# Moving the low parts of two projection weights to GpSimd, with a new front order, in a fused attention and MoE kernel

## The chip, the cores and the metric

The kernel runs on one core of one Trainium2 chip. Its time is the device time of one execution in microseconds (us). Three runs took 939.1, 931.1 and 933.65 us, so the median is 933.65. A separate profiled execution took 935.56 us, of which the profile's span covers 933.7.

## The reference

```
xn = layernorm(x)                              # x: 4 x 512 tokens x 512
p  = xn @ W_in.T ; s_t = d*s_(t-1) + (1-d)*p_t # d = sigmoid(decay), a scan over tokens
a  = s @ W_out.T + bias
r  = softmax(xn @ wg_router.T)                 # 32 experts, top 6, weights renormalised
y  = sum over the chosen experts of w * (silu(xn@w_gate[e]) * (xn@w_up[e])) @ w_down[e]
sh = (silu(xn@ws_gate) * (xn@ws_up)) @ ws_down # shared expert, width 704
out = x + a + y + sh
```

## The kernel before, in words

**Split matmuls.** Every product is computed with three matmuls: an fp32 operand v is split into a high part (v rounded to fp32r, written by ACT as a copy) and a low part (v less the high part, a subtraction on DVE), and TensorE (PE) adds high x high, high x low and low x high. All copies share the profile's line L859, all subtractions L1573, and the three matmuls are L1256, L1257 and L1258. The profile names a buffer by its memory: `w_hi` also stands for the high parts of the projection weights, of the normalised input `xb` and of the scanned states `st`.

**The front** (0 to about 112 us). The 2,048 tokens are 16 tiles of 128 rows, and four batches of 4 tiles. Per tile: DVE measures mean and variance (`measure`, L1596 and L1599), ACT takes the root (`deviation`, L879), DVE the factors (`factors`, L1605 and L1606), ACT writes normalised rows for the transposes (`normalise`, L885) and a second, reordered copy for HBM (`reorder`, L893), PE transposes (`tile_T`, L1236), and DVE moves the result to SBUF (`tile_evac`, L1586). Per batch: ACT and DVE split the input (`xb_hi`, `xb_lo`), PE projects four column chunks (`in_proj`), ACT scales each (`q`, into two buffers), DVE scans it (`scan_of`, L1845), ACT and DVE split the states (`st_hi`, `st_lo`), and PE projects out (`out_proj`). Both projection weights are split by `wT_hi` (ACT) and `w_lo_T` (DVE), four chunks each. `xb` is one buffer: `xb_hi(1)` waits until all of `in_proj(0)` is done.

**The order is written out by hand** on each engine, each of which works strictly in order and waits on semaphores. `in_proj(b)` chunk m waits for `q` of two chunks earlier.

**Units.** After the front come 8 shared half passes (units 0 to 6 and the last) and 32 experts in order of load (SH = 7 is the first, rank 0). A unit is gate/up (three chunks), then down. In the shared units DVE also does the routing steps, a table `routing` by unit: order of the experts, slots, `shift(k)` (nine steps that compact token positions; L1695 to L1698), `segments`, row tables, extra blocks.

**Gathers and quarter moves.** For an expert GpSimd gathers its tokens by indirect DMAs (L769), `quarters` rearranges them with 16 small DMAs (L520), and DVE transposes 32x32 squares (`squares`, L1954), ACT and DVE split them, and PE starts when all blocks are split. For the first expert, 8 of the 16 quarter moves are issued by SP and 8 by ACT; for all others SP issues all 16. SP reaches them after the stores and loads of shared tiles 8 to 15 (L617 and L527), and ACT after a copy of the expert's down weights.

Of the kernel before, what the change touches and what calls it, by code (L numbers as in the profile page):

```python
# [200 lines left out]
def build(nc, x, w_in, w_out, decay, bias, wg, w_gate, w_up, w_down, ws_gate, ws_up, ws_down, out,  # L201
          xn_rows, table):
    with ExitStack() as ctx:
# [285 lines left out]
        def xb_of(b):  # L489
            return xb if b < B - 1 else (xT_hi[0], xT_lo[0])  # L490
# [34 lines left out]
        def _(sp):  # L525
# [118 lines left out]
            quarters(sp, SH, range(QUARTERS // 2))  # L644
# [40 lines left out]
        def _(pool):  # L685
# [13 lines left out]

            io(iota_e[:], [[1, E]], 0, 0)  # L700
# [31 lines left out]

            pool.wait_ge(s_x0[TILES - 1], 16)
# [119 lines left out]
        def _(act):  # L853
# [145 lines left out]
            xb_hi(0)  # L999
            deviation(4)  # L1000
            reorder(0)
            reorder(1)
            normalise(4)
            normalise(5)
            wT_hi(1, 0)
            wT_hi(1, 1)
            wT_hi(1, 2)
            deviation(6)
            wT_hi(1, 3)
            normalise(6)  # L1010
            normalise(7)
            q(0, 0)
            q(0, 1)
            deviation(8)
            reorder(2)
            st_hi(0, [0])
            reorder(3)
            normalise(8)
            q(0, 2)
            st_hi(0, [1])  # L1020
            normalise(9)
            q(0, 3)
            st_hi(0, [2])
            xb_hi(1)
# [92 lines left out]
            for u in range(UNITS):  # L1117
# [3 lines left out]
                if u == SH - 1:  # L1121
                    w_hi_piece(SH, GATE)
                    w_hi_piece(SH, UP)
                    silu(3 * u)
                    h_hi(3 * u)
                    w_hi_piece(SH, WIDE_GU)
                    silu(3 * u + 1)
                    h_hi(3 * u + 1)
                    w_hi_piece(SH, DOWN)
                    quarters(act, SH, range(QUARTERS // 2, QUARTERS))  # L1130
                    for t in range(blocks(SH)):
                        xt_hi(SH, t)
                    silu(3 * u + 2)
                    w_hi_piece(SH, NARROW_GU)
                    h_hi(3 * u + 2)
                    continue
# [90 lines left out]
        def _(pe):  # L1227
# [44 lines left out]
            def in_proj_first():  # L1272

                w, x = w_inT, xb_of(0)
                for c in range(DC):
                    pe.wait_ge(s_wth, c + 1)
                    pe.wait_ge(s_xbh, c + 1)
                    t_.matmul(p_gu[0][:], w[0][:, c, 0:P], x[0][:, c, :], start=(c == 0), stop=False)
                for c in range(DC):
                    pe.wait_ge(s_wT, c + 1)  # L1280
                    t_.matmul(p_gu[0][:], w[1][:, c, 0:P], x[0][:, c, :], start=False, stop=False)
                for c in range(DC):
                    pe.wait_ge(s_xb, c + 1)
                    mm = t_.matmul(p_gu[0][:], w[0][:, c, 0:P], x[1][:, c, :], start=False,
                                   stop=(c == DC - 1))
                mm.then_inc(s_in, 1)

            def in_proj(b, chunks=range(DC)):
                for m in chunks:
                    if DC * b + m >= 2:  # L1290
                        pe.wait_ge(s_q, DC * b + m - 1)
                    for c in range(DC):
                        if m == 0 and b > 0:
                            pe.wait_ge(s_xb, DC * b + c + 1)
                        mm = three(p_gu[m % 2][:], [w[:, c, m * P:(m + 1) * P] for w in w_inT],
                                   [v[:, c, :] for v in xb_of(b)], c == 0, c == DC - 1)
                    mm.then_inc(s_in, 1)
# [30 lines left out]
            in_proj_first()  # L1328
            in_proj(0, [1])
# [233 lines left out]
        def _(dve):  # L1563
# [267 lines left out]
            def w_lo_T(i, c):  # L1831
                dve.wait_ge(s_wth, DC * i + c + 1)
                low((w_inT, w_outT)[i][1][:, c, :], nat[i][:, c, :], (w_inT, w_outT)[i][0][:, c, :]
                    ).then_inc(s_wT, 1)

# [28 lines left out]
            w_lo_T(0, 0)  # L1864
            w_lo_T(0, 1)
            w_lo_T(0, 2)
            w_lo_T(0, 3)
            measure(4)
            xb_lo(0)
            factors(4)  # L1870
            measure(6)
            tile_evac(4)
            factors(6)
            w_lo_T(1, 0)
            tile_evac(5)
            measure(8)
            scan_of(0, 0)
            scan_of(0, 1)
            factors(8)
            st_lo(0, [0])  # L1880
            tile_evac(6)
            tile_evac(7)
            scan_of(0, 2)
            st_lo(0, [1])
            tile_evac(8)
            tile_evac(9)
            xb_lo(1)
# [4 lines left out]
            scan_of(0, 3)  # L1892
            st_lo(0, [2])
            w_lo_T(1, 1)
            w_lo_T(1, 2)
            tile_evac(10)
            tile_evac(11)
            w_lo_T(1, 3)
# [37 lines left out]
            w_lo_piece(0, DOWN)  # L1936
            constants()
            load_order()
            st_lo(3)
            shift(3)  # L1940
# [69 lines left out]
            def end_weights(u):  # L2010
# [7 lines left out]
                0: (expert_order, main_slots, extra_slots, lambda: shift(4)),  # L2018
                1: (lambda: shift(5), lambda: shift(6)),
                2: (lambda: shift(7), lambda: shift(8), segments),  # L2020
                3: (main_rows, extra_rows, lambda: extra_experts(0), lambda: extra_experts(TILES)),
                4: (lambda: extra_experts(2 * TILES), lambda: extra_experts(3 * TILES), extra_blocks),
# [164 lines left out]
```

## Time and profile before

| | |
|---|---|
| median of three runs | 933.65 us (931.1 to 939.1) |
| profiled execution | 935.56 us, span 933.7 us |
| PE busy | 910.3 us, 97% of the span |
| DVE, ACT, POOL busy | 644.4, 520.7, 389.4 us |
| HBM read and written | 121.16 and 42.61 MB |

"Busy" is the time in which an engine has an instruction running. Matmuls overlap, so a busy PE row of 0.39 us starts every 0.23 us. An engine's idle time stands in brackets behind the instruction that ended it, with the instruction that released it.

### The profile page before, as it was taken

What the parts mean: (1) busy time and instruction counts of PE and PEld (TensorE: products, weight loads), DVE (VectorE), ACT (ScalarE), POOL (GpSimd) and SP (SyncE); (2) the same over time, 40 slices, a digit from 0 to 9 for tenths busy, and PEclk for the clock granted to TensorE, in tenths of its full rate; (3) what the DMA queues carried; (4) which work ended last, traced back from release to release, by engine and by line L of the source; (5) the groups of instructions that cost most, each with busy time, mean ns of one, the idle gap of its engine ahead of it and who ended that gap; (6) DMA issues with size and microseconds to landing.
All of it is one profiled execution on the core that took longest, in us unless ns stands there. A gap on an engine that the chain in (4) does not pass through costs nothing.

```text
span 933.7 us, 13995 instructions
## 1 busy us (share of the span) xinstructions
PE 910.3 (97%) x4480; PEld 808.2 (87%) x4480; DVE 644.4 (69%) x1140; ACT 520.7 (56%) x877; POOL 389.4 (42%) x318
## 2 busy tenths in 40 slices
PE   7899999999998999999999999999999999999997
PEld 6768877888887899999999999999999899998885
DVE  6868858656446777677777667766767667658665
ACT  7984541212134665666665666766666567557561
POOL 3001000010301556666767665666457546555321
PEclk9999999999999999999999999999999999999999
DMA  8352254222544999989899899899999999999855
GB/s 332 138 192 102 89 194 139 90 60 94 173 126 118 300 250 237 242 237 259 219 232 230 232 235 264 235 231 233 281 245 233 255 259 247 243 246 275 194 111 124
DMA packets 127723, 191.30 MB, mean 205 GB/s; under 512 B 16384, under 2 KB 73488, under 8 KB 127392
## 3 DMA queue, kind: packets, MB, share of 16 engines
q1 hardware_dynamic: 102480, 132.56, 45.2%
q0 software_dynamic: 23856, 57.29, 29.7%
q8 instruction: 37, 0.61, 0.3%
q10 hardware_dynamic: 1312, 0.53, 0.2%
q14 instruction: 38, 0.31, 0.1%
HBM read 121.16 MB, written 42.61 MB: 175 GB/s over the span
## 4 chain that ended last, share of the span: by engine, by line
PE 58%; DMA 10%; SPq 8%; DVE 7%; issue 6%; ACT 5%; POOL 4%; POOLq 1%; ACTq 1%; DVEq 0%
PE p_gu L1256 11%; PE p_gu L1258 11%; PE p_gu L1257 11%; SPq L520 8%; DMA xnT<-xn_rows,ids 6%; PE p_y L1256 6%; PE p_y L1257 6%; PE p_y L1258 6%; DMA xnT<-xnT 2%; POOL xnT L769 2%; POOL out L783 2%; DVE w_lo L1573 2%; DMA xnT<-xn_rows 1%; ACT w_hi L859 1%; PE p_gu L1378 1%
## 5 line engine op out<-in xcount | busy, mean ns | idle before, releaser
L783 POOL DMA_INDIRECT out<-rows,ids x112 | 200.9, 1794 | 218.2 <-ACT rows L859 193.9
L1256 PE MATMUL p_gu<-xT_hi,w_hi 128*128 128x512 f32 (+12 forms) x816 | 287.5, 352 | 2.9 <-DVE xT_lo L1573 2.9
L1258 PE MATMUL p_gu<-xT_hi,w_lo 128*128 128x512 f32 (+12 forms) x816 | 287.2, 352 | 0.0
L1257 PE MATMUL p_gu<-xT_lo,w_hi 128*128 128x512 f32 (+12 forms) x816 | 287.1, 352 | 0.0
L769 POOL DMA_INDIRECT xnT<-xn_rows,ids x112 | 163.2, 1457 | 110.1 <-DVE xT_lo L1573 45.3
L1573 DVE TENSOR_TENSOR w_lo<-raw,w_hi 128x1024 fp32r<-128x1024 f32 (+2 forms) x148 | 173.7, 1178 | 9.6 <-ACT w_hi L859 9.6
L1256 PEld LDWEIGHTS p_gu<-xT_hi,w_hi 128*128 128x128 f32 x816 | 153.7, 188 | 14.9 <-DVE xT_lo L1573 3.3
L1257 PEld LDWEIGHTS p_gu<-xT_lo,w_hi 128*128 128x128 f32 x816 | 153.8, 189 | 11.5
L1258 PEld LDWEIGHTS p_gu<-xT_hi,w_lo 128*128 128x128 f32 x816 | 153.6, 188 | 7.9
L859 ACT ACTIVATE w_hi<-raw 128x1024 fp32r<-128x1024 f32 (+2 forms) x148 | 151.3, 1027 | 2.8 <-PE p_gu L1258 2.1
L1256 PE MATMUL p_y<-w_hi,hT_hi 128*128 128x512 f32 (+1 forms) x368 | 145.1, 394 | 4.9 <-ACT rows L859 2.2
L1257 PE MATMUL p_y<-w_lo,hT_hi 128*128 128x512 f32 (+1 forms) x368 | 144.3, 392 | 0.0
L1258 PE MATMUL p_y<-w_hi,hT_lo 128*128 128x512 f32 (+1 forms) x368 | 144.0, 391 | 0.0
L859 ACT ACTIVATE hT_hi<-h_sb 128x384 fp32r<-128x384 f32 (+8 forms) x120 | 64.8, 540 | 123.8 <-DVE h_sb L1791 99.0
L1791 DVE TENSOR_TENSOR h_sb<-sg,p_gu 128x512 f32<-128x512 f32 (+12 forms) x84 | 48.7, 579 | 113.3 <-PE p_gu L1258 106.7
L914 ACT ACTIVATE sg<-p_gu 128x512 f32<-128x512 f32 (+22 forms) x120 | 61.7, 514 | 111.5 <-PE p_gu L1258 111.2
L1954 DVE STREAM_TRANSPOSE xT_raw<-xnT 128x512 f32<-128x512 f32 x116 | 75.8, 654 | 26.2 <-DMA xnT<-xnT 24.8
L859 ACT ACTIVATE xT_hi<-xT_raw 128x512 fp32r<-128x512 f32 (+3 forms) x116 | 67.4, 581 | 45.4 <-DVE xT_raw L1954 43.5
L1573 DVE TENSOR_TENSOR hT_lo<-h_sb,hT_hi 128x384 fp32r<-128x384 f32 (+8 forms) x116 | 66.2, 570 | 31.0 <-ACT hT_hi L859 31.0
L1256 PEld LDWEIGHTS p_y<-w_hi,hT_hi 128*128 128x128 f32 (+1 forms) x368 | 69.1, 188 | 20.6 <-issue 3.1
L1258 PEld LDWEIGHTS p_y<-w_hi,hT_lo 128*128 128x128 f32 (+1 forms) x368 | 69.1, 188 | 15.0
L1257 PEld LDWEIGHTS p_y<-w_lo,hT_hi 128*128 128x128 f32 (+1 forms) x368 | 69.2, 188 | 11.0
(227 smaller groups left out, 1050.8 us busy)
## 6 DMA issues: line engine op xcount, KB each, us to landing
raw<-L_ffn_w_gate SPq DMA_DIRECT2D x32, 704.0 KB, 5.6
raw<-L_ffn_w_up SPq DMA_DIRECT2D x32, 704.0 KB, 7.9
xnT<-xnT SPq DMA_DIRECT2D x424, 48.0 KB
raw<-L_ffn_w_down SPq DMA_DIRECT2D x32, 512.0 KB, 8.5
raw<-L_ffn_w_down SPq DMA_DIRECT2D x32, 192.0 KB, 9.5
xring<-out SPq DMA_DIRECT2D x20, 256.0 KB, 3.5
out<-xring SPq DMA_DIRECT2D x20, 256.0 KB, 2.4
xnT<-xnT SPq DMA_DIRECT2D x80, 64.0 KB
```

The costliest lines, as they stand in the source:

```text
L520: queue.dma_start(xq[par][a_ * SQ:(a_ + 1) * SQ, 0:n, b, :], xe[b * SQ:(b + 1) * SQ, 4 * par:4 * par + n, a_ * P:(a_ + 1) * P]).then_inc(s ...
L769: pool.indirect_dma_start(out=xe[0:n, 4 * x_half(u) + t, :], out_offset=None, in_=xn_rows[:, :], in_offset=bass.IndirectOffsetOnAxis(ap=id ...
L783: pool.indirect_dma_start(out=out[:, :], in_=y_sb[t][0:n, :], in_offset=None, out_offset=bass.IndirectOffsetOnAxis(ap=ids[0:n, col:col + 1 ...
L859: return a.activation(dst, src, ACT.Copy, scale=scale)
L914: a.activation(sg[0:k, 0:n], p_gu[2 * q % 3][0:k, 0:n], ACT.Silu).then_inc(s_sg, 1)
L1256: t_.matmul(dst, stat[0], mov[0], start=first, stop=False)
L1257: t_.matmul(dst, stat[0], mov[1], start=False, stop=False)
L1258: return t_.matmul(dst, stat[1], mov[0], start=False, stop=last)
L1378: mm = t_.matmul(dst[:, 0:n], w_nar[:, s, kc, :], x[1][:, kc, 0:n], start=False, stop=(kc == DC - 1))
L1573: return v.tensor_tensor(dst, src, hi, ALU.subtract)
L1791: v.tensor_tensor(h_sb[0:k, 0:n], sg[0:k, 0:n], p_gu[(2 * q + 1) % 3][0:k, 0:n], ALU.mult).then_inc(s_h, 1)
L1954: v.transpose(xT_raw[x_half(u)][:, :, t * P:t * P + n].rearrange("p s (b j) -> p b s j", j=SQ), xq[x_half(u)][:, t, 0:n // SQ, :].rearrang ...
```

## The change

GpSimd computes all eight low parts of the two projection weights; the four of W_in come in its program before its constants, the four of W_out before it zeroes rows in HBM. The first chunk of every batch's `in_proj` runs its four high x high matmuls first, then those with the low weight, then those with the low input (before, only batch 0 did). SP issues all 16 quarter moves of the first expert. The orders of ACT and DVE in the first part of the front are written anew. `st_lo(3)` comes ahead of the routing constants and the load order, and the routing steps are dealt out to the shared units differently.

```
-            quarters(sp, SH, range(QUARTERS // 2))
+            quarters(sp, SH)
@@ gpsimd
+            def w_lo_T(i, c):
+                pool.wait_ge(s_wth, DC * i + c + 1)
+                g.tensor_tensor((w_inT, w_outT)[i][1][:, c, :], nat[i][:, c, :], (w_inT, w_outT)[i][0][:, c, :],
+                                ALU.subtract).then_inc(s_wT, 1)
+            for c in range(DC):
+                w_lo_T(0, c)
             io(iota_e[:], [[1, E]], 0, 0)
...
+            for c in range(DC):
+                w_lo_T(1, c)
             pool.wait_ge(s_x0[TILES - 1], 16)
@@ scalar, the front: see the rows of the order below
             xb_hi(0)
+            reorder(0)
             deviation(4)
-            reorder(0)
-            reorder(1)
...
@@ scalar, unit SH - 1
                     w_hi_piece(SH, DOWN)
-                    quarters(act, SH, range(QUARTERS // 2, QUARTERS))
@@ tensor
-            def in_proj_first():
+            def in_proj_high_first(b):
...
+                    if m == 0:
+                        in_proj_high_first(b)
+                        continue
@@ vector, the front: see the rows of the order below
             tile_evac(3)
-            w_lo_T(0, 0)
...
-            measure(4)
             xb_lo(0)
+            measure(4)
...
@@ vector, after scan_of(3, 3) and w_lo_piece(0, DOWN)
+            st_lo(3)
             constants()
             load_order()
-            st_lo(3)
-            shift(3)
             mult(0)
@@ vector
             routing = {
-                0: (expert_order, main_slots, extra_slots, lambda: shift(4)),
-                1: (lambda: shift(5), lambda: shift(6)),
-                2: (lambda: shift(7), lambda: shift(8), segments),
-                3: (main_rows, extra_rows, lambda: extra_experts(0), lambda: extra_experts(TILES)),
-                4: (lambda: extra_experts(2 * TILES), lambda: extra_experts(3 * TILES), extra_blocks),
+                0: (expert_order, lambda: shift(3)),
+                1: (main_slots, lambda: shift(4), lambda: shift(5)),
+                2: (lambda: shift(6), lambda: shift(7), lambda: shift(8), segments),
+                3: (extra_slots, main_rows, extra_rows, lambda: extra_experts(0)),
+                4: (lambda: extra_experts(TILES), lambda: extra_experts(2 * TILES), lambda: extra_experts(3 * TILES), extra_blocks),
             }
```

**ACT, from `q(0, 1)` on, before.** `std` is a deviation, `rows<-later_71` a normalise, `w_hi<-scan` an `st_hi`, `w_hi<-xnT` the `xb_hi` of batch 1, `w_hi<-raw` a `wT_hi` of W_out:

```order
L859 ACTIVATE q_sb<-p_gu,dec 128x512 x2
L879 ACTIVATE std<-mv,epst 128x2
L893 ACTIVATE by_quarter<-first_70,nmr,rstd 128x512
L859 ACTIVATE w_hi<-scan 128x512
L893 ACTIVATE by_quarter<-first_70,nmr,rstd 128x512
L885 ACTIVATE rows<-later_71,nmr,rstd 128x512
L859 ACTIVATE q_sb<-p_gu,dec 128x512
L859 ACTIVATE w_hi<-scan 128x512
L885 ACTIVATE rows<-later_71,nmr,rstd 128x512
L859 ACTIVATE q_sb<-p_gu,dec 128x512
L859 ACTIVATE w_hi<-scan 128x512
L859 ACTIVATE w_hi<-xnT 128x512 x4
```

And now, from `deviation(8)` to the same point (lines are those of the changed kernel, 9 higher here):

```order
L888 ACTIVATE std<-mv,epst 128x2
L868 ACTIVATE w_hi<-raw 128x512 x2
L894 ACTIVATE rows<-later_71,nmr,rstd 128x512
L868 ACTIVATE q_sb<-p_gu,dec 128x512
L894 ACTIVATE rows<-later_71,nmr,rstd 128x512
L868 ACTIVATE w_hi<-xnT 128x512 x4
L868 ACTIVATE q_sb<-p_gu,dec 128x512
L868 ACTIVATE w_hi<-scan 128x512
L902 ACTIVATE by_quarter<-first_70,nmr,rstd 128x512
L868 ACTIVATE w_hi<-raw 128x512 x2
L902 ACTIVATE by_quarter<-first_70,nmr,rstd 128x512
L868 ACTIVATE w_hi<-scan 128x512 x2
```

The first state copy of batch 0 stood ahead of `xb_hi(1)` and three chunks of states were copied by then. Now the first one stands behind `xb_hi(1)` and `q(0, 3)`, and four copies of W_out stand in this stretch.

**DVE at the same place, before.** `w_lo<-scan` is an `st_lo`, `w_lo<-xnT` the `xb_lo` of batch 1:

```order
L1845 SCALAR_TENSOR_TENSOR scan<-dec,q_sb 128x512 x2
L1605 RECIPROCAL rstd<-std 128x2
L1606 SCALAR_TENSOR_TENSOR nmr<-mv,rstd 128x2
L1573 TENSOR_TENSOR w_lo<-scan,w_hi 128x512
L1586 COPY xnT<-p_tx 128x4x128
L1586 COPY xnT<-p_gu 128x4x128
L1845 SCALAR_TENSOR_TENSOR scan<-dec,q_sb 128x512
L1573 TENSOR_TENSOR w_lo<-scan,w_hi 128x512
L1586 COPY xnT<-p_tx 128x4x128
L1586 COPY xnT<-p_gu 128x4x128
L1573 TENSOR_TENSOR w_lo<-xnT,w_hi 128x512 x4
```

And now:

```order
L1847 SCALAR_TENSOR_TENSOR scan<-dec,q_sb 128x512
L1603 BN_STATS stats<-later_71 128x6 x2
L1606 BN_AGGR mv<-stats 128x2 x2
L1612 RECIPROCAL rstd<-std 128x2
L1613 SCALAR_TENSOR_TENSOR nmr<-mv,rstd 128x2
L1580 TENSOR_TENSOR w_lo<-scan,w_hi 128x512
L1847 SCALAR_TENSOR_TENSOR scan<-dec,q_sb 128x512
L1580 TENSOR_TENSOR w_lo<-xnT,w_hi 128x512 x4
L1847 SCALAR_TENSOR_TENSOR scan<-dec,q_sb 128x512
L1580 TENSOR_TENSOR w_lo<-scan,w_hi 128x512
L1593 COPY xnT<-p_tx 128x4x128
L1593 COPY xnT<-p_gu 128x4x128
```

`xb_lo(1)` used to come behind two `st_lo` that ACT had served, and the four evacuations. Now it stands behind the first `st_lo` and a scan, and the `st_lo` needs the copy that ACT makes behind `xb_hi(1)`. The evacuations of tiles 8 and 9 and `measure(10)` stand behind all of it.

## Rows read from the trace of the kernel before

**Rows 1.** Engine busy time by stretch: start and end, busy, then PE, PEld, DVE, ACT, POOL with counts, clock, DMA share, GB/s.
```profile
25.00:50.00 25.00, 23.04 (x103) 19.11 (x104) 22.69 (x45) 23.77 (x34) 0.00 (x0) 0.93 0.33 120
...
250.00:300.00 50.00, 47.08 (x207) 39.59 (x207) 26.17 (x40) 17.40 (x28) 9.34 (x13) 0.97 0.47 133
...
400.00:500.00 100.00, 100.00 (x502) 93.44 (x501) 71.63 (x128) 63.91 (x119) 68.35 (x50) 1.00 0.90 231
```

**Rows 2.** Timeline of PE: start, duration, line, operation, tiles, shapes, count, idle time and releaser.
```profile
25.28 0.75 PE L1236 MATMUL p_tx<-ident,rows 128*128 128x128 f32 x4 [1.42 <-ACT rows L885]
...
27.68 0.63 PE L1256 MATMUL p_gu<-w_hi 128*128 128x512 f32 x1
...
33.50 0.39 PE L1258 MATMUL p_gu<-w_hi,w_lo 128*128 128x512 f32 x1
...
36.53 0.47 PE L1256 MATMUL p_gu<-w_hi 128*128 128x512 f32 x1 [1.68 <-DVE w_lo L1573]
...
45.69 0.48 PE L1256 MATMUL p_gu<-w_hi 128*128 128x512 f32 x1
...
118.02 0.50 PE L1256 MATMUL p_y<-w_hi 128*128 128x512 f32 x1 [0.61 <-DVE w_lo L1573]
...
152.56 0.50 PE L1256 MATMUL p_y<-w_hi,hT_hi 128*128 128x512 f32 x1 [1.56 <-DVE hT_lo L1573]
...
286.91 0.74 PE L1256 MATMUL p_gu<-xT_hi,w_hi 128*128 128x448 f32 x1 [2.92 <-DVE xT_lo L1573]
```

**Rows 3.** Timeline of ACT in the front and at the first shared unit.
```profile
13.58 2.18 ACT L859 ACTIVATE w_hi<-xnT 128x512 fp32r<-128x512 f32 x4
...
37.12 2.50 ACT L893 ACTIVATE by_quarter<-xring,nmr,rstd 128x512 f32<-128x512 f32 x2
...
42.06 2.94 ACT L885 ACTIVATE rows<-later,nmr,rstd 128x512 f32<-128x512 f32 x4 [0.24 <-DVE nmr L1606]
...
140.16 0.60 ACT L914 ACTIVATE sg<-p_gu 128x512 f32<-128x512 f32 x1 [1.55 <-PE p_gu L1258]
```

**Rows 4.** Timeline of DVE in the front.
```profile
15.66 1.28 DVE L1596 BATCH_NORM_STATS2 stats<-xring 128x6 f32<-128x512 f32 x2
...
23.42 0.69 DVE L1586 COPY xnT<-p_tx 128x512 f32<-128x512 f32 x1 [2.06 <-PE p_tx L1236]
...
26.98 2.31 DVE L1845 TENSOR_TENSOR_SCAN scan<-dec,q_sb 128x512 f32<-128x512 f32 x2
```

**Rows 5.** Timeline of GpSimd (POOL) in its set-up.
```profile
2.10 0.51 POOL L693 MEMSET raw<- 128x512 f32 x1
...
7.08 0.24 POOL L731 TENSOR_TENSOR by_e<-same_e,iota_e 128x32 f32<-128x32 f16 x1
```

**Rows 6.** Timeline of DVE from the last scan to the first unit's routing.
```profile
115.47 2.50 DVE L1573 TENSOR_TENSOR w_lo<-scan,w_hi 128x512 fp32r<-128x512 f32 x4
...
117.89 0.29 DVE L1695 TENSOR_SCALAR moves<-step 128x512 int16<-128x512 int16 x1
...
119.58 0.69 DVE L1791 TENSOR_TENSOR h_sb<-sg,p_gu 128x512 f32<-128x512 f32 x1
...
143.11 2.23 DVE L1738 SCALAR_TENSOR_TENSOR r<-r 128x32 f32<-128x32 f32 x10
...
149.54 0.69 DVE L1791 TENSOR_TENSOR h_sb<-sg,p_gu 128x512 f32<-128x512 f32 x1
```

**Rows 7.** Timeline of the SP queue, then of ACT and DVE, at the first expert's quarter moves.
```profile
274.11 6.43 SPq L520 DMA_DIRECT2D xnT<-xnT  x9
...
279.95 6.37 SPq L520 DMA_DIRECT2D xnT<-xnT  x10
...
274.93 5.82 ACTq L520 DMA_DIRECT2D xnT<-xnT  x7
...
282.30 1.31 DVE L1954 STREAM_TRANSPOSE xT_raw<-xnT 128x512 f32<-128x512 f32 x2 [4.57 <-DMA xnT<-xnT]
...
293.99 0.71 DVE L1954 STREAM_TRANSPOSE xT_raw<-xnT 128x512 f32<-128x512 f32 x1
```

More of the change, by code:

```diff
@@ L999, in _ @@
             xb_hi(0)
+            reorder(0)
             deviation(4)
-            reorder(0)
-            reorder(1)
             normalise(4)
             normalise(5)
+            deviation(6)
+            normalise(6)
+            q(0, 0)
+            normalise(7)
+            q(0, 1)
+            reorder(1)
+            deviation(8)
             wT_hi(1, 0)
             wT_hi(1, 1)
[L1007 to L1017, printed above, removed]
             normalise(8)
             q(0, 2)
-            st_hi(0, [1])
             normalise(9)
+            xb_hi(1)
             q(0, 3)
-            st_hi(0, [2])
-            xb_hi(1)
+            st_hi(0, [0])
+            reorder(2)
+            wT_hi(1, 2)
+            wT_hi(1, 3)
+            reorder(3)
+            st_hi(0, [1, 2])
             reorder(4)
@@ L1270, in totals @@
                           ).then_inc(s_tot, 1)
-            def in_proj_first():
-                w, x = w_inT, xb_of(0)
+            def in_proj_high_first(b):
+                w, x = w_inT, xb_of(b)
                 for c in range(DC):
                     pe.wait_ge(s_wth, c + 1)
-                    pe.wait_ge(s_xbh, c + 1)
+                    pe.wait_ge(s_xbh, DC * b + c + 1)
                     t_.matmul(p_gu[0][:], w[0][:, c, 0:P], x[0][:, c, :], start=(c == 0), stop=False)
@@ L1282, in in_proj_first @@
                 for c in range(DC):
-                    pe.wait_ge(s_xb, c + 1)
+                    pe.wait_ge(s_xb, DC * b + c + 1)
                     mm = t_.matmul(p_gu[0][:], w[0][:, c, 0:P], x[1][:, c, :], start=False,
@@ L1291, in in_proj @@
                         pe.wait_ge(s_q, DC * b + m - 1)
+                    if m == 0:
+                        in_proj_high_first(b)
+                        continue
                     for c in range(DC):
-                        if m == 0 and b > 0:
-                            pe.wait_ge(s_xb, DC * b + c + 1)
                         mm = three(p_gu[m % 2][:], [w[:, c, m * P:(m + 1) * P] for w in w_inT],
@@ L1327, in _ @@
             keep_running(10)
-            in_proj_first()
-            in_proj(0, [1])
+            in_proj(0, [0, 1])
             tile_T(4)
@@ L1829, in xg_lo @@
                 low(xT_lo[i % 2][:], xnT[:, BATCH[i]], xT_hi[i % 2][:]).then_inc(s_xt, 1)
[L1831 to L1834, printed above, removed]
             def xb_lo(b, chunks=range(DC)):
@@ L1863, in _ @@
             tile_evac(3)
-            w_lo_T(0, 0)
-            w_lo_T(0, 1)
-            w_lo_T(0, 2)
-            w_lo_T(0, 3)
+            xb_lo(0)
             measure(4)
-            xb_lo(0)
             factors(4)
             measure(6)
+            factors(6)
             tile_evac(4)
-            factors(6)
-            w_lo_T(1, 0)
             tile_evac(5)
+            scan_of(0, 0)
+            tile_evac(6)
+            tile_evac(7)
+            scan_of(0, 1)
             measure(8)
-            scan_of(0, 0)
-            scan_of(0, 1)
             factors(8)
             st_lo(0, [0])
-            tile_evac(6)
-            tile_evac(7)
             scan_of(0, 2)
+            xb_lo(1)
+            scan_of(0, 3)
             st_lo(0, [1])
@@ L1886, in _ @@
             tile_evac(9)
-            xb_lo(1)
             measure(10)
@@ L1891, in _ @@
             factors(12)
-            scan_of(0, 3)
             st_lo(0, [2])
-            w_lo_T(1, 1)
-            w_lo_T(1, 2)
             tile_evac(10)
             tile_evac(11)
-            w_lo_T(1, 3)
             st_lo(0, [3])
```

## The prediction

> **What bounds the kernel now.** I read the busy time by stretch first. From 400 to 500 us PE is busy all 100 us at a granted clock of 1.00 (the upper level, 2.4 GHz) [rows 1]: in the experts nothing can be won without fewer matmuls, and the change removes none. Time can only come from PE's idle gaps before about 300 us, and any time that PE loses there is passed on whole, since later work runs back to back. PE's timeline gives the gaps that the change can touch [rows 2]: 1.42 us before a transpose at 25.28, 1.68 at 36.53, 0.61 at 118.02, 1.56 at 152.56, and 2.92 at 286.91. The first matmuls after the gap at 25.28 are slow: one takes 0.63 us at 27.68 where 0.39 is usual [rows 2], in a stretch whose mean granted clock is 0.93 [rows 1]. Eight such matmuls start 0.43 apart instead of 0.23, which is 1.6 us. Each gap in the front is released by ACT or DVE [rows 2]; so there the order of the work on ACT and DVE sets the time, and their two timelines are the views to read.
>
> **Routing steps, the first unit: -1.6 us.** The gap at 152.56 waits for DVE. There `silu` was ready at 140.76 [rows 3], but the product that uses it starts at 149.54, behind the routing steps [rows 6]. The change takes main slots, extra slots and one shift out (143.11 to 149.54 less one shift, which stays: 6.43 - 1.7 = 4.7 us [rows 6]), so the low part that PE waits for is 4.7 us earlier and the whole 1.56 goes. The steps land in units 1 to 4. Unit 1 gains 1.6 us, unit 2 gains one shift (1.7), unit 3 some 0.8 and unit 4 1.4 us. In these units PE does 12 down matmuls and 12 gate matmuls (5.4 us at 0.23) between the chunk that feeds the late product and the matmul that needs it, so I count them as nothing; if that cover were gone they would cost 1 to 2 us each.
>
> **`st_lo(3)` first: -0.6 us.** PE waits at 118.02 for the last subtraction of a group that begins at 115.47, behind the load order [rows 6]. The group takes 2.50 us, and without the load order ahead of it it ends well before PE arrives at 118.02 - 0.61 = 117.4. The gap goes (the other end of this term is 0, if ACT's copies were late). The load order then ends about where the group did, and the shift of 1.7 us (117.89 to 119.58) is no longer ahead of the next product [rows 6]: nothing is late.
>
> **Quarter moves: +3.6 us.** SP's first stretch shows 9 moves in 6.43 us beside ACT's queue, and 10 in 6.37 us when ACT's queue is done, 0.64 apart [rows 7]. ACT ends its part at 274.93 + 5.82 = 280.75, and DVE can start on the squares at 282.30, 1.55 later [rows 7]. Alone, SP issues 16 from 274.11 on: 15 x 0.64 + 0.6 = 10.2 us, to 284.3, and DVE starts at 285.85. That is 3.55 us later, and PE waits on this very chain: the gap of 2.92 before 286.91 [rows 2] grows to about 6.5. SP does not come there earlier, because it stands behind the stores and loads of shared tiles. ACT, freed of 8 issues, has nothing to do but wait for the squares. Queued behind on SP are the moves of the second expert; they would end at 294.5 and land near 296, and DVE wants them at 293.99 + 3.6 = 297.6 [rows 7], so that is hidden. The bounds: 0, if SP alone could issue at the rate that both make together (16 in 6.6 us), and 5.1, eight moves at 0.64. The row for SP alone decides for 3.6.
>
> **The front: +2.0 us, and 0.8 for the clock.** I went through both engines in the new order with the distances between starts in the old rows: ACT copy 0.52 (2.18 for four), reorder 1.20 (2.50 for two), normalise 0.71 (2.94 for four) [rows 3]; DVE subtraction or evacuation 0.60, scan 1.14 (2.31 for two), a measure of two tiles 1.5 [rows 4, 6].
>
> - `xb_lo(0)` follows ACT's copies from 14.2 to 16.7. ACT's last four copies of W_in stand right ahead of 13.58 [rows 3], so the first is ready at 12.1, and GpSimd's four subtractions run from there. For their price no row stands: a GpSimd fill of 512 columns takes 0.51 and a two-input operation on 32 columns 0.24 [rows 5], so 0.5 is one end and 0.24 x 16 = 3.9 the other. I take 1.1, twice the fill, as it has the same length and two inputs. The last is then ready at 16.6, and PE wants it at 16.9: hidden. The Trainium skill, page "GPSIMD Engine Reference", section 3.1, has a two-input operation at 1.96 times DVE's time; that would be 1.2 us each and leave the sum as it is.
> - PE ends `in_proj(0)` at 29.6 where it ended at 33.9 [rows 2]. So far 4.3 us are won, part of it the slow matmuls.
> - They are lost again. `measure(8)` now stands behind `scan_of(0, 1)` and ends at 27.7, and ACT, with `deviation(8)` next, idles from 25.0. It reaches `xb_hi(1)` at 31.0 and the first state copy at 33.7. DVE waits for that copy from 28.4 to 34.3, then scans, and `xb_lo(1)` runs from 36.1 to 38.5. PE has its high parts done at 34.2 and waits until 36.8. The first chunk of batch 1 ends at 38.9, where it ended 2.7 us after 36.53 [rows 2]: the lead is 0.4.
> - ACT comes to `reorder(4)` at 38.7, not 37.12 [rows 3]. DVE does `measure(10)` and `measure(12)` only then, to 44.5; ACT waits for them, and its four normalises start at 44.8, not 42.06 [rows 3]. `q(1, 1)` stands behind them, and PE's last chunk of batch 1 waits for it: 48.4, not 45.69 [rows 2]. PE is 2.7 behind.
> - The high-first order of batch 2 gives back 0.7, since PE no longer waits for each low part in turn. At the router's matmuls PE is 2.0 behind, and after them it has no gap until 118.02.
>
> Bounds: 0 (the high-first order and a quicker DVE hide it) to 2.7. PE idles before 48.4 for 1.0 and 1.4 us. Such a gap was followed by the lower level of the clock once [rows 2] and not at 36.53, so I take half of 1.6, 0.8, with ends 0 and 1.6.
>
> **The sum.** -1.6 - 0.6 + 3.6 + 2.0 + 0.8 = +4.2 us. On the profiled execution's 935.6 us that is 939.8; it stands 1.9 above the median of 933.65, so for the median I say **938**. GpSimd zeroes its rows in HBM behind the last low part of W_out, at about 38 in my walk, and the evacuation of tile 12, at about 58, is the first to need it: three DMAs in 20 us, which I count as nothing.
>
> **Rivals.**
>
> *The port.* GpSimd's subtractions and DVE's two-input subtractions run at the same time twice: 14.2 to 16.7 on `xb_lo(0)`, and about 36 to 38.5 on `xb_lo(1)`, where `wT_hi(1, 2)` and `(1, 3)` have just been made. If one blocks the other, each DVE subtraction waits up to 1.1 us: 2.2 us at the first place, up to 2.2 at the second, and both stand on the chain that I followed. That gives some 3 us more, 941. The Trainium skill, page "SBUF — State Buffer", section "Who interferes with whom", says that a DVE instruction with two SBUF inputs contends with a GpSimd instruction that reads SBUF, and that the later one is blocked whole. No row of this trace has the two side by side, so nothing here speaks for or against it. Chance 0.30.
>
> *The lead stays: faster.* The 4.3 us at the end of `in_proj(0)` are kept. It decides at PE's first matmul of batch 1: it must come before 32, and `q(1, 1)` must be done before 41.5. Then -4.3 - 2.2 + 3.6 = -2.9, or 931. For it: DVE has 4.8 us less to do (eight subtractions at 0.60 [rows 6]), and PE's gap at 36.53 is a wait for DVE [rows 2]. Against it: DVE waits in order for ACT's state copy. Chance 0.12.
>
> *GpSimd is slow.* At 3.9 us each the fourth low part is ready at 27.7, and PE is 10.8 us late there: 949. Chance 0.05.
>
> *Nothing adds up:* the front comes out even and the quarter moves cost what the routing gives back. 933 to 935, chance 0.08.
>
> **Chances and range.** My forecast (slower by 2 to 6 us) has 0.45. Under 1% (9.3 us) a measurement of this kernel can hardly tell from no change, its own three runs being 8 us apart. Only the slow GpSimd, and the port with a slow clock on top, go past that: slower by over 1% has 0.13, faster 0.03, within 1% 0.84. The range takes in the forecast with its bounds, most of the port case and the even case: 931.5 to 945.
>
> **What would show it.** In the profile after: PE's gap before the first expert's gate at 6 to 7 us, released by `xT_lo`, and 16 moves on SP only. No gap before the fourth out projection and before unit 0's last down chunk. ACT idle some 2.7 us before `deviation(8)`, DVE idle some 6 us before its first `st_lo`, and PE's first chunk of batch 1 done at about 39, its last begun at about 48. GpSimd's subtractions at about 1.1 us; DVE's beside them at 0.69, or stretched if the port counts. The forecast is wrong if SP's 16 moves are done in under 8 us, or if PE starts batch 1's last chunk before 46.

## The result, and the profile after

| | before | changed |
|---|---|---|
| median, us | 932.72 (4 runs, 931.1 to 939.1) | 943.5 (4 runs, 940.71 to 945.81) |
| ratio | 1 | 1.0102, 95% interval 1.0065 to 1.0139 |
| profiled execution, its span | 935.56, 933.7 | 940.71, 939.0 |

The changed kernel is slower by 10.8 us between the medians. The forecast was 938, or +4.2 us: the sign is right and the median lies in the stated range (931.5 to 945), but the loss is over twice the forecast. The profiled execution is the fastest of the four, so the two traces explain 5.3 us of span; what the other 5.5 are, no trace shows.

Engine busy time by stretch, first of the changed kernel (stretch, its length, PE, PEld, DVE, ACT, POOL with counts, clock, DMA share, GB/s):

```profile
25.00:50.00 25.00, 20.17 (x71) 14.87 (x71) 18.08 (x33) 18.95 (x28) 8.34 (x7) 0.80 0.36 134
...
100.00:200.00 100.00, 100.00 (x443) 82.52 (x442) 68.37 (x123) 33.93 (x49) 1.82 (x2) 1.00 0.36 121
...
250.00:300.00 50.00, 42.92 (x183) 35.58 (x182) 23.29 (x34) 12.82 (x20) 11.23 (x14) 0.93 0.45 123
```

and the stretch of the kernel before that [rows 1] lacks:

```profile
100.00:200.00 100.00, 97.83 (x431) 80.06 (x430) 65.25 (x128) 30.63 (x43) 3.60 (x5) 1.00 0.35 120
```

From 100 to 200 us the 2.17 us of idle time are gone. From 250 to 300 PE is busy 4.2 us less than in [rows 1]. From 25 to 50 it is busy 2.9 us less, and the mean granted clock is 0.80 where it was 0.93.

PE's timeline of the changed kernel:

```profile
26.53 0.63 PE L1264 MATMUL p_gu<-w_lo,w_hi 128*128 128x512 f32 x1
...
32.98 0.39 PE L1265 MATMUL p_gu<-w_hi,w_lo 128*128 128x512 f32 x1
...
39.25 0.49 PE L1291 MATMUL p_gu<-w_lo,w_hi 128*128 128x512 f32 x1 [2.06 <-DVE w_lo L1580]
40.95 0.80 PE L1291 MATMUL p_gu<-w_lo,w_hi 128*128 128x512 f32 x1 [1.20 <-DVE w_lo L1580]
42.64 1.40 PE L1291 MATMUL p_gu<-w_lo,w_hi 128*128 128x512 f32 x2 [0.90 <-DVE w_lo L1580]
43.83 0.63 PE L1263 MATMUL p_gu<-w_hi 128*128 128x512 f32 x1
...
52.87 0.50 PE L1263 MATMUL p_gu<-w_hi 128*128 128x512 f32 x1 [1.10 <-ACT q_sb L868]
...
69.84 3.64 PE L1252 MATMUL p_y<-xnT,wgT 128*32 128x512 f32 x32
...
294.83 0.74 PE L1263 MATMUL p_gu<-xT_hi,w_hi 128*128 128x448 f32 x1 [7.08 <-DVE xT_lo L1580]
```

The router's matmuls, the mark behind the front, stood here before:

```profile
63.25 3.64 PE L1245 MATMUL p_y<-xnT,wgT 128*32 128x512 f32 x32
```

So PE is 6.6 us late behind the front, where the forecast had 2.8. There is no gap of over 0.15 us between there and 294.83; those of 118.02 and 152.56 [rows 2] are gone. The gap at the first expert grew from 2.92 to 7.08 us. In the front PE waits three times in a row for `xb_lo(1)`, 4.16 us together, and slow matmuls (0.63) stand from 26.5 to 29.1 and from 43.8 to 46. The last matmul of `in_proj(0)` ends at 32.98 + 0.39 = 33.4; before it was 33.9, and the walk had 29.6.

ACT's timeline of the changed kernel, in the front:

```profile
20.48 0.30 ACT L888 ACTIVATE std<-mv,epst 128x2 f32<-128x2 f32 x1 [3.84 <-DVE mv L1606]
...
29.86 0.30 ACT L888 ACTIVATE std<-mv,epst 128x2 f32<-128x2 f32 x1 [2.56 <-DVE mv L1606]
...
33.47 2.19 ACT L868 ACTIVATE w_hi<-xnT 128x512 fp32r<-128x512 f32 x4 [0.28 <-PE p_gu L1265]
```

DVE's, in the front and at the first expert's squares:

```profile
13.89 5.07 DVE L1580 TENSOR_TENSOR w_lo<-xnT,w_hi 128x512 fp32r<-128x512 f32 x4 [0.88 <-ACT w_hi L868]
...
36.79 0.69 DVE L1580 TENSOR_TENSOR w_lo<-scan,w_hi 128x512 fp32r<-128x512 f32 x1 [6.24 <-ACT w_hi L868]
...
38.53 4.65 DVE L1580 TENSOR_TENSOR w_lo<-xnT,w_hi 128x512 fp32r<-128x512 f32 x4
...
290.22 1.30 DVE L1947 STREAM_TRANSPOSE xT_raw<-xnT 128x512 f32<-128x512 f32 x2 [8.73 <-DMA xnT<-xnT]
```

GpSimd's:

```profile
11.94 5.88 POOL L702 TENSOR_TENSOR w_lo<-raw,w_hi 128x512 fp32r<-128x512 f32 x4 [9.31 <-ACT w_hi L868]
...
30.76 2.55 POOL L702 TENSOR_TENSOR w_lo<-raw,w_hi 128x512 fp32r<-128x512 f32 x2 [8.22 <-ACT w_hi L868]
...
38.56 3.47 POOL L702 TENSOR_TENSOR w_lo<-raw,w_hi 128x512 fp32r<-128x512 f32 x2 [5.25 <-ACT w_hi L868]
```

Here is what decides this case. The pair at 30.76 runs alone, at 1.27 us each. The groups at 11.94 and 38.56 run beside DVE's two-input subtractions of 13.89 and 38.53, and then both are long: DVE's four take 5.07 and 4.65 us, where four took 2.50 [rows 6]. The view of one buffer's instructions gives the single durations (minimum, median and maximum in ns, first and last start), here at the first place and then at the second:

```profile
L702 POOL TENSOR_TENSOR w_lo<-raw,w_hi x4: 1275/1496/1733, 11.9 to 16.1; 128x512 fp32r<-128x512 f32 x4
L1580 DVE TENSOR_TENSOR w_lo<-xnT,w_hi x4: 679/1423/1773, 13.9 to 18.3; 128x512 fp32r<-128x512 f32 x4
...
L702 POOL TENSOR_TENSOR w_lo<-raw,w_hi x2: 1723/1752/1780, 38.6 to 40.3; 128x512 fp32r<-128x512 f32 x2
L1580 DVE TENSOR_TENSOR w_lo<-xnT,w_hi x4: 668/1224/1775, 38.5 to 42.5; 128x512 fp32r<-128x512 f32 x4
```

SP's queue at the first expert:

```profile
277.87 2.53 SPq L520 DMA_DIRECT2D xnT<-xnT  x3
...
279.32 19.84 SPq L520 DMA_DIRECT2D xnT<-xnT  x30
```

These are issues 0.73 apart at first, then 0.66. From the first issue to the squares it is 290.22 - 277.87 = 12.35 us, and was 282.30 - 274.11 = 8.19 [rows 7].

### The profile page after: what moved, and what is told of

It reads as the page before. It is cut to its first block, busy times and chain, and to the rows that moved or that the text cites. A ratio compares the mean times of both kernels' runs of the same rounds, so it can differ in the third digit from the quotient of the medians.

```text
span 939.0 us, 14002 instructions
## 1 busy us (share of the span) xinstructions
PE 913.3 (97%) x4480; PEld 809.8 (86%) x4480; DVE 644.8 (69%) x1132; ACT 521.5 (56%) x877; POOL 402.4 (43%) x326
## 4 chain that ended last, share of the span: by engine, by line
PE 67%; SPq 9%; DMA 7%; issue 5%; DVE 5%; POOL 3%; ACT 3%; POOLq 1%; DVEq 0%; ACTq 0%
PE p_gu L1263 13%; PE p_gu L1264 13%; PE p_gu L1265 13%; SPq L520 8%; PE p_y L1263 7%; PE p_y L1264 7%; PE p_y L1265 7%; DMA xnT<-xn_rows,ids 4%; DMA xnT<-xnT 2%; PE p_gu L1385 1%; PE p_gu L1383 1%; POOL xnT L778 1%; POOL out L792 1%; PE p_y L1463 1%; PE p_y L1465 1%
## 5 line engine op out<-in xcount | busy, mean ns | idle before, releaser
L1580 DVE TENSOR_TENSOR w_lo<-raw,w_hi 128x1024 fp32r<-128x1024 f32 (+2 forms) x140 | 168.6, 1206 | 9.6 <-ACT w_hi L868 9.6
```

What stands on the lines that cost most here:

```text
L1580: return v.tensor_tensor(dst, src, hi, ALU.subtract)
```

## Experiments

Every ratio is to the kernel before, timed in the same chip session, with its 95% interval.

### The three parts, one at a time

**only_quarters.** The kernel before, with the quarter moves changed:

```diff
-            quarters(sp, SH, range(QUARTERS // 2))
+            quarters(sp, SH)
...
-                    quarters(act, SH, range(QUARTERS // 2, QUARTERS))
```

> The kernel before with the quarter moves of the first expert all on SP, nothing else. Theory (SP's issue time is on the path): PE's gap before the first expert's gate grows from 2.9 us to 6.5 to 7.1 us, all of it stays to the end, and the time is 3.6 to 4.2 us above before. Rival (two queues only share one rate, so SP alone is as fast): the gap stays at about 3 us and the time is equal. Second rival (the later experts absorb it): the gap grows, and less than half of it is left in the time.

Measured: 938.99 us against 933.81, ratio 1.0052 (1.0031 to 1.0073). Its PE timeline has the gap of the changed kernel, and the stretch 250 to 300 shows the slow matmuls behind it in the clock:

```profile
291.02 0.74 PE L1255 MATMUL p_gu<-xT_hi,w_hi 128*128 128x448 f32 x1 [7.17 <-DVE xT_lo L1572]
```

```profile
250.00:300.00 50.00, 42.83 (x181) 35.66 (x180) 20.70 (x32) 13.90 (x23) 9.24 (x13) 0.90 0.44 126
```

The part costs 4.9 us by the ratio (2.9 to 6.8 by its interval): 4.25 more of gap, and a stretch at 0.90 where [rows 1] has 0.97. That the slow matmuls make up the rest is likely, but lies within the interval.

**only_routing.** The kernel before, with the routing steps and `st_lo(3)` changed:

```diff
+            st_lo(3)
...
-            st_lo(3)
-            shift(3)
...
-                0: (expert_order, main_slots, extra_slots, lambda: shift(4)),
+                0: (expert_order, lambda: shift(3)),
+                1: (main_slots, lambda: shift(4), lambda: shift(5)),
...
```

> The kernel before with only st_lo(3) ahead of the load order and the routing steps dealt out anew. Theory: the two gaps of PE, 0.6 us before the fourth out projection and 1.6 us before unit 0's last down chunk, are gone, no new one appears in units 1 to 4, and the time is 2.2 us below before. Rival (the steps push a product of units 1 to 4 onto the path): new gaps there and no gain.

Measured: 931.02 us, ratio 0.9964 (0.9945 to 0.9984), 3.4 us faster. Both gaps are gone (2.17 us), and no gap came in their place before the first expert.

**only_front.** The kernel before, with GpSimd's subtractions, the new orders of ACT and DVE and the high-first matmuls, without the other two parts:

```diff
-            w_lo_T(0, 0)
-            w_lo_T(0, 1)
-            w_lo_T(0, 2)
-            w_lo_T(0, 3)
+            xb_lo(0)
...
+                    if m == 0:
+                        in_proj_high_first(b)
+                        continue
...
```

> The kernel before with GpSimd's low parts, the new orders of ACT and DVE and the high-first chunks, but with the old routing and the old quarter moves. Theory (the new order makes ACT and DVE wait for each other, and the port doubles DVE's xb_lo): the router's matmuls begin at about 69.8 us as in the changed kernel and not at 63.3, and the time is 6 to 7 us above before. Rival (the front's loss is won back behind the router, where other engines have slack): the router is late by 6 us, the time is less than 3 us above before.

Measured: 940.87 us, ratio 1.0071 (1.0043 to 1.0098), 6.6 us slower. The router's matmuls begin at 69.75, as in the changed kernel, behind the same three waits:

```profile
39.13 0.50 PE L1292 MATMUL p_gu<-w_lo,w_hi 128*128 128x512 f32 x1 [2.04 <-DVE w_lo L1581]
40.83 0.79 PE L1292 MATMUL p_gu<-w_lo,w_hi 128*128 128x512 f32 x1 [1.19 <-DVE w_lo L1581]
42.52 1.39 PE L1292 MATMUL p_gu<-w_lo,w_hi 128*128 128x512 f32 x2 [0.89 <-DVE w_lo L1581]
```

**undo_quarters.** The changed kernel, with the moves split over SP and ACT again:

```diff
-            quarters(sp, SH)
+            quarters(sp, SH, range(QUARTERS // 2))
...
+                    quarters(act, SH, range(QUARTERS // 2, QUARTERS))
```

> The changed kernel with the quarter moves split between SP and ACT as before. Theory (the parts add up): front +6.6, routing -2.2, so 4 to 5 us above before and about 4 us below the changed kernel; gap before the first expert about 3 us. Rival (the time of the changed kernel over 943 comes from something later than the first expert, since its profiled run ended only 5.3 us late): still over 940.

Measured: 938.92 us, ratio 1.0049 (1.0029 to 1.0069). The gap at the first expert is 2.96 us. The three parts sum to 0.0052 - 0.0036 + 0.0071 = 0.0087, inside the interval of the whole (0.0065 to 0.0139): nothing speaks against their adding, and the front is the largest.

### What in the front costs it

**old_order_gpsimd.** The kernel before, with only the engine of the eight weight subtractions changed; they leave DVE's list, and all else keeps its place:

```diff
+            for c in range(DC):
+                w_lo_T(0, c)
...
+            for c in range(DC):
+                w_lo_T(1, c)
...
-            w_lo_T(0, 0)
...
```

> The kernel before with all eight low parts of the projection weights on GpSimd and taken out of DVE's order, the orders of ACT and DVE otherwise untouched, in_proj as before. Theory (the new order did the harm, the move by itself does little): measure(4) comes between on DVE, so the port costs xb_lo(0) at most 1 to 2 us; the router begins within 1 us of 63.3 and the time is between 2 us below and 1 us above before. Rival (the port is the cause): the router is late by 3 us or more and the time too.

Measured: 933.67 us, ratio 1.0009 (0.9986 to 1.0031), router's matmuls at 62.46 (63.25 in the kernel before, and 62.05 in `only_routing`, whose front is the same as before). DVE's single durations beside GpSimd show contention for `xb_lo(0)` here too, and none at `xb_lo(1)`, by which time GpSimd has nothing left to do:

```profile
L1582 DVE TENSOR_TENSOR w_lo<-xnT,w_hi x4: 677/878/1785, 15.5 to 18.8; 128x512 fp32r<-128x512 f32 x4
```

```profile
34.92 2.48 DVE L1582 TENSOR_TENSOR w_lo<-xnT,w_hi 128x512 fp32r<-128x512 f32 x4
```

**new_order_dve.** The new orders and the high-first matmuls, with the subtractions on DVE, each beside the work that it feeds:

```diff
+            w_lo_T(0, 0)
...
+            w_lo_T(0, 3)
             xb_lo(0)
             measure(4)
...
             factors(8)
+            w_lo_T(1, 0)
+            w_lo_T(1, 1)
             st_lo(0, [0])
...
             factors(12)
+            w_lo_T(1, 2)
+            w_lo_T(1, 3)
             st_lo(0, [2])
```

> The new front order and the high-first chunks, but with all eight low parts on DVE (the four of W_in before xb_lo(0), two of W_out after factors(8), two before the third st_lo); old routing, old quarter moves. DVE does 2.4 us more ahead of measure(4) and 1.2 us in the gap where it idles. Theory (the order is at fault, the port adds 2.7 and 2.2 us): xb_lo takes 2.5 us for four again, not 5.1 and 4.7, the router begins at 66 to 68 us, and the time is 3 to 5 us above before, 2 to 3 below the kernel with the same order and GpSimd. Rival (the order is good, the port alone is at fault): router at 63 or earlier, no loss.

Measured: 937.55 us, ratio 1.0034 (1.0014 to 1.0055), router's matmuls at 67.62. DVE's timeline: still idle before the first `st_lo`, and `xb_lo(1)` at the late place, but at its old duration. PE waits once and not three times:

```profile
36.73 0.69 DVE L1572 TENSOR_TENSOR w_lo<-scan,w_hi 128x512 fp32r<-128x512 f32 x1 [4.39 <-ACT w_hi L859]
...
38.48 2.47 DVE L1572 TENSOR_TENSOR w_lo<-xnT,w_hi 128x512 fp32r<-128x512 f32 x4
```

```profile
39.20 2.31 PE L1283 MATMUL p_gu<-w_lo,w_hi 128*128 128x512 f32 x4 [2.06 <-DVE w_lo L1572]
```

Against the kernel before, the router's matmuls are 4.4 us late here, 6.5 in `only_front`, and not late with GpSimd in the old order. The two new-order runs reach `xb_lo(1)` within 0.1 us of each other (38.48 and 38.41). From there the group takes 2.47 us in one and 4.65 in the other, and the router's matmuls are 2.1 us apart. That is the price of contention there, on the chain that PE waits for. By the times the difference is 0.0071 - 0.0034 = 0.0037, from two sessions and with intervals that overlap, so it rests on the rows.

The 4.4 us are not the price of the order alone. In this run DVE does the four subtractions of W_in ahead of `xb_lo(0)`:

```profile
14.41 2.49 DVE L1572 TENSOR_TENSOR w_lo<-raw,w_hi 128x512 fp32r<-128x512 f32 x4
16.81 2.49 DVE L1572 TENSOR_TENSOR w_lo<-xnT,w_hi 128x512 fp32r<-128x512 f32 x4
```

It is through with both at 19.3, and the changed kernel with its one stretched group at 13.89 + 5.07 = 19.0; `xb_lo(1)` then begins at 38.48 here and at 38.53 there. So at the first place contention took about what the move of W_in's subtractions had freed. No run has the new order with neither.

**measure_first.** The changed kernel, with `measure(4)` ahead of `xb_lo(0)` on DVE:

```diff
+            measure(4)
             xb_lo(0)
-            measure(4)
```

> The changed kernel with measure(4) ahead of xb_lo(0) on DVE, so that DVE runs operations with one input in SBUF beside GpSimd's two-input subtractions first. Theory (only DVE operations with two inputs in SBUF and GpSimd's reads shut each other out): the two BN_STATS take 0.64 us each beside GpSimd; GpSimd's subtractions beside them take 1.27 us like alone, xb_lo(0) takes about 3 us for four instead of 5.1, ACT's deviation(4) comes at about 16 us instead of 20.5 and the time is 2 to 4 us below the changed kernel. Rival (any DVE work beside GpSimd is slowed): BN_STATS stretched to over 1 us each.

Measured: 941.05 us, ratio 1.0081 (1.0049 to 1.0112), router's matmuls at 69.01. `deviation(4)` comes earlier, but `factors(4)`, now behind the stretched group, holds ACT for 2.52 us. `xb_lo(1)` is as long as before, and 0.8 us is won of the 6.6 at the router's matmuls, where 2 to 4 of time were expected. What did come as expected is which operations are stretched: `measure(4)`, whose operations read one operand, runs beside GpSimd's first subtractions and takes 1.28 us for two, as it did in [rows 4], and the group of two-operand subtractions behind it is stretched:

```profile
13.26 1.28 DVE L1603 BATCH_NORM_STATS2 stats<-xring 128x6 f32<-128x512 f32 x2
...
14.73 4.62 DVE L1580 TENSOR_TENSOR w_lo<-xnT,w_hi 128x512 fp32r<-128x512 f32 x4
```

**xb_lo_first.** One group moved on DVE in the changed kernel:

```diff
             factors(8)
-            st_lo(0, [0])
             scan_of(0, 2)
             xb_lo(1)
+            st_lo(0, [0])
             scan_of(0, 3)
```

> The changed kernel, with one group moved on VectorE: the four x_lo subtractions of batch 1 (xb_lo(1)) stand ahead of the first st_lo, not behind it; nothing else differs. Theory (the front's loss beyond the port is this place in the order): in the changed kernel VectorE idles 6.24 us before the st_lo at 36.79, because its st_hi comes behind xb_hi(1) and q on ScalarE, while the four x_hi it could work on are there from 33.47 on. Moved ahead, x_lo(1) runs at about 34.0 to 36.7, alone, since GpSimd's pair ends at 33.3; TensorE's three waits (2.06, 1.20, 0.90) and most of the slow matmuls after them go, so the router's matmuls begin at 64.8 to 65.8 and not at 69.84, and the ratio is about 1.005 (1.0035 to 1.0065) where the change has 1.010. Rival (the two engines' contention is the whole loss, wherever the group stands): x_lo(1) takes 4 us or more again, the router begins after 68, and the ratio stays at 1.008 or above.

Measured: 940.88 us against 935.41, ratio 1.0062 (1.0040 to 1.0084), router's matmuls at 66.79. The first part of the theory holds: the group runs alone at its old duration, and PE's three waits for it are gone. The second doesn't: PE reaches the next chunk early and waits there for ACT's `q_sb`, which stands behind reorders, W_out copies and state copies. The mark came 1 us later than expected, 3.05 us earlier than in the changed kernel; the ratio's interval overlaps the change's, so this too rests on the rows.

```profile
34.70 2.46 DVE L1580 TENSOR_TENSOR w_lo<-xnT,w_hi 128x512 fp32r<-128x512 f32 x4
```

```profile
44.29 0.80 PE L1263 MATMUL p_gu<-w_hi 128*128 128x512 f32 x1 [3.43 <-ACT q_sb L868]
```

### The first expert's moves, issued early

**early_quarters.** The kernel before with the routing part, and all sixteen moves on SP ahead of the stores of shared tiles 8 to 11:

```diff
+                if g == B - 1:
+                    quarters(sp, SH)
                 for t in range(TPB * (g - 1), TPB * g):
                     store_shared(t)
...
-            quarters(sp, SH, range(QUARTERS // 2))
```

> The kernel before with the new routing, and with all 16 quarter moves of the first expert on SP ahead of the stores of shared tiles 8 to 11, where SP is idle. Theory (the gap before the first expert is the issue time of moves that begin too late, not data that is late): the moves run from about 257 to 268 us, DVE turns the squares right behind the split of the down weights, PE's gap of 2.9 us and the slow matmuls behind it (1.5 us) go, and the time is 2.5 us (routing) plus 3 to 4.4 us below before, 926 to 928. Rival (something else of the first expert is late next, its weights or the gather): a gap of 1 us or more stays and less than 2 us are won beyond routing.

Measured: 926.05 us against 934.0, ratio 0.9916 (0.9890 to 0.9942). SP issues the moves at 248.75, at the same price each, and PE is busy for the whole stretch:

```profile
248.75 10.47 SPq L520 DMA_DIRECT2D xnT<-xnT  x16
```

```profile
250.00:300.00 50.00, 50.00 (x229) 42.73 (x228) 32.14 (x50) 20.81 (x34) 7.91 (x11) 1.00 0.52 147
```

So the changed kernel's 12.35 us at this place are SP's, and they cost nothing once they lie beside the shared expert's matmuls.

**early_after.** The same edit in the changed kernel.

> The changed kernel, with the first expert's sixteen moves issued by SyncE ahead of the stores of shared tiles 8 to 11, and not behind the loads of the shared tiles 12 to 15. Theory (the parts add): the 7.08 us gap at the first expert and the slow matmuls after it are gone; from the change's 1.010, 0.005 for the quarter moves and another 0.005 for the gap that the kernel before had there (early moves and routing 0.9916 against routing alone 0.9964) go, so the ratio is 0.999 to 1.001, and what is left of a loss is the front's. Rival (a later wait takes it back in this order of routing steps and front): 1.004 or more.

Measured: 933.9 us against 935.41, ratio 0.9977 (0.9955 to 0.9999). There is no gap at the first expert, and the router's matmuls still begin at 69.49. It came out a little below the expected 0.999 to 1.001: what the early moves win, the gap of the kernel before included, pays for the front.

**early_xb_lo_first.** Both edits.

> Both edits at once in the changed kernel. If they are independent, their gains add: ratio 0.993 to 0.997, router's matmuls at 65 to 66, no gap at the first expert. If the front's loss were hidden by or moved into a later wait, it would come no lower than early moves alone, 0.999 or more.

Measured: 929.7 us, ratio 0.9939 (0.9915 to 0.9963), as expected of independent edits. The router's matmuls begin at 66.75, as with `xb_lo_first` alone and again later than the expected 65 to 66.

**early_high_first.** `early_quarters` with the high-first matmuls, in the old orders:

```diff
-            in_proj_first()
-            in_proj(0, [1])
+            in_proj(0, [0, 1])
...
+                    if m == 0:
+                        in_proj_high_first(b)
+                        continue
```

> A try at the fastest version: the kernel before with the routing steps spread, the sixteen moves early, and of the front change only the order of matmuls in the first chunk of every batch (all x_hi products, then those with w_lo, then x_lo); ScalarE's, VectorE's and GpSimd's order of before. In the same kernel without that matmul order TensorE waits 1.75 and 1.44 us for x_lo of batches 1 and 2, with x_hi there. Theory: the eight matmuls ahead of x_lo (1.84 us at full clock) cover those waits, the router's matmuls begin 1.5 to 3 us earlier than 61.9, and the ratio falls from 0.992 to 0.988 to 0.990. Rival: TensorE then waits for ScalarE's q or rows in place of x_lo, and the ratio stays at 0.991 to 0.993.

Measured: 926.22 us, ratio 0.9898 (0.9873 to 0.9923). PE's gaps for `x_lo` of batches 1 and 2 (1.75 and 1.44 us) are gone, and one of 0.96 for ACT's `x_hi` is there. The router's matmuls begin at 62.35, not earlier than the 61.88 without the edit; this execution's first transposes of tile 4 came 1 us later. Its ratio can't be told from `early_quarters`' 0.9916. So the expected 1.5 to 3 us did not come. Either version is some 0.8 to 1.0% faster than the kernel before.

## Why the prediction was right or wrong

**Routing and `st_lo(3)`: right.** Forecast -2.2; the two gaps lose 2.17 us of idle time, and alone the part gives -3.4 (1.5 to 5.1 by its interval). The later units hid the steps, as counted.

**Quarter moves: right in mechanism, a little small.** Forecast +3.6. The gap grew by 4.16, because SP's first moves take 0.73 each, not 0.64, and DVE's squares follow the last issue a little later. The slow matmuls after a gap of 7 us, which the sum left out, are the likely rest of the 4.9 by time. The second expert's moves behind them cost nothing, as said.

**The front: wrong in size, and this is where the sum was wrong.** It had +2.0, and 0.8 for the clock; rows give 6.6 at the router's matmuls, and `only_front` 6.6 by time. The mis-sized step is the price of DVE's subtractions beside GpSimd's:

- *The port, 4.6 us.* I had put DVE's subtractions beside GpSimd at their old price, and the port among the rivals with 0.30. It came true at both places named: 5.07 us and 4.65 us for four. A DVE subtraction beside GpSimd takes up to 1.77 us where 0.68 is its own, which is most of one GpSimd subtraction (1.27 alone) more, and GpSimd's rise to 1.78 as well. The walk had `xb_lo(1)` from 36.1 to 38.5; it ran from 38.53 to 43.2. Its late start, 2.4 us, comes from the first place: `xb_lo(0)` ended at 19.0 and not 16.7, `measure(4)` stood behind it and ACT idled 3.84 us before `deviation(4)`, and `xb_hi(1)` began at 33.47 and not 31.0. The other 2.2 are the second place. So the lead of 4.3 us at the end of `in_proj(0)`, with which the walk went on, was 0.5: 2.2 less by the late rows of ACT, and 1.6 by eight slow matmuls. The second place is shown by `only_front` against `new_order_dve`; the first is read from the rows against the walk. The Trainium skill, page "SBUF — State Buffer", section "Who interferes with whom", has a DVE instruction with two SBUF inputs contend with a GpSimd instruction that reads SBUF; the trace agrees, and its durations (1.77 against 0.68) show what it costs here.
- *The order: near the forecast.* The chain was the one forecast: ACT idle before `deviation(8)` (2.56, forecast 2.7), DVE idle before its first `st_lo` (6.24, forecast some 6), normalises and the last chunk of batch 1 late. Behind `xb_lo(1)` the marks are late by one amount against the walk: the last chunk of batch 1 begins at 52.87 and not 48.4, the router's matmuls at 69.84 and not 63.25 + 2.0 = 65.25. That is 4.5 and 4.6 us, the port's. The 4.4 us of `new_order_dve` fit too, 2.0 and the 2.4 that DVE's four subtractions take there. No run shows the 2.0 by itself. `xb_lo_first` shows that the place of the `st_lo` ahead of `xb_lo(1)` is a link of the chain, and that ACT's place for `q(1, 0)` is the next.
- *The clock, forecast 0.8: hardly anything at the router's matmuls.* The slow matmuls were there (14 at about 0.63, and 0.80 for the stretch 25 to 50, where the row before has 0.93 [rows 1]), but waits hid them: after the first group `xb_hi(1)` waits 0.28 us for PE, and after the second PE still waits 1.10 us for `q_sb` at 52.87. Four executions with this front had the router's matmuls at 69.84, 69.75, 69.95 and 69.49 (`only_front`, `undo_quarters` and `early_after` behind the first), the first with 0.80 in that stretch and the others with 0.86. Where the clock does count is in the kernel before: against its front at a clock of 1.00 (62.05 in `only_routing`) the new one is 7.8 us late.

GpSimd's own price was near: 1.27 us alone, taken as 1.1. PE did wait for it in the first batch, 1.13 us where I had it hidden, since beside DVE four took 5.88 us; but `old_order_gpsimd` is even in time, so the engine alone was not the loss.

**The rivals.** *The port* came true, above its price: 2.2 us at each place were written down and "some 3" taken for both, and both came whole. *The lead stays* fell: PE's first matmul of batch 1 came at 34.2, not before 32. *GpSimd is slow* (3.9 us each) fell at 1.27. *Nothing adds up* fell on the front alone. The case past 1% (0.13) can't be decided: the kernel is 1.02% slower, with an interval of 0.65 to 1.39%. Its condition, the port with a slow clock on top, held only in the port. For the profiled execution the forecast was 939.8, and 940.71 came; that nearness is luck, for at the first expert the loss was 7.9 us and not 4.2, and part of it went away later.

**A part of the loss is taken back late.** At the first expert the changed kernel is 294.83 - 286.91 = 7.9 us behind, at the end 5.3. The groups of PE's down matmuls from 300 us on (time busy, mean ns, then the idle time before them and the parts of it by releaser) tell most of why, in the kernel before:

```profile
L1256 PE MATMUL p_y<-w_hi,hT_hi 128*128 128x512 f32 (+1 forms) x296 | 116.8, 395 | 3.3 <-ACT rows L859 2.2 <-DVE hT_lo L1573 0.6
```

and in the changed one:

```profile
L1263 PE MATMUL p_y<-w_hi,hT_hi 128*128 128x512 f32 (+1 forms) x300 | 118.0, 393 | 1.2 <-ACT rows L868 0.8
```

The idle time before these matmuls was 2.1 us longer in this execution of the kernel before, 1.4 of it waits for ACT's `rows`. It doesn't go with the change: `undo_quarters` has 3.6 us at the same place, `only_quarters` 1.6.

## What to carry to other kernels

When work is moved from DVE to GpSimd, list what DVE does in the same microseconds: two-input operations of both on SBUF stretch each other, and it costs as much as lies on the chain that PE waits for, so the same move was even in one order, and in the other one stretched group alone cost 2.1 us. In an in-order engine's list, look at what an early waiting step keeps from running (here four subtractions whose inputs were ready), and on removing it name the next wait before counting the gain. A serial issue of many small DMAs is worth moving in time rather than between queues: ahead of the stores it cost nothing, and with the new routing steps it made the kernel 0.8% faster than before, where the routing alone gave 0.4%.

## What the runs showed of the hardware

- A GpSimd subtraction of 128x512 f32 takes 1.27 us alone (2.55 for two), and up to 1.78 beside DVE's two-input subtractions; DVE's take 0.68 alone and up to 1.77 beside it. DVE's BN_STATS, with one input, took no longer beside GpSimd (1.28 for two).
- SP issues these quarter moves 0.65 to 0.66 us apart alone (16 in 10.47 us, 30 in 19.84).
- The clock after a gap is not the same each time: after the same wait for `rows` before the transposes of tile 4 (1.41 or 1.42 us) the stretch 25 to 50 ran at 0.93 in the kernel before and at 1.00 in `only_routing`, which is the same program up to there. That is 1.2 us at the router's matmuls (63.25 and 62.05), so a part of any difference of this size in the front is chance.
